# Attention block on one core: the fourth head's probabilities turned by DMA, a ring of five x buffers, the turned norm copied by VectorE

## The chip, the cores and the metric

The kernel runs on one core of a Trainium2 chip. The metric is the device time of one execution in microseconds (us); the value shown is the median of several executions. One more execution was recorded by the hardware profiler, and all rows below come from it.

## What is computed

The input is x, 32 batches of 256 rows by 512, and adj, 32 batches of 256 by 256. For each batch, with 16 heads of width 32:

```
h = max(layernorm(x), 0)
q, k, v = h @ Wq.T, h @ Wk.T, h @ Wv.T            (split into 16 heads)
a = q k^T * 512**-0.5 + 2 * adj                    (per head, 256 x 256)
a = where(any(a != 0, axis=-1), a, -inf); p = softmax(a); p = where(isnan(p), 0, p)
out = x + concat(p v) @ Wo.T
```

The weights are 512 by 512. All data is fp32.

## The kernel before

**The slots.** A batch is called a slot of the pipeline and is cut into 16 steps, one per head (line 541 for ScalarE, 546 and on; each engine has its own `slot` function, and `run`, line 290, calls it for every batch). In a slot the heads of the current batch (`t.cur`) go through softmax, the projections of the next batch (`t.nxt`) are made, and the last group of heads and the output projection of the batch before (`t.prev`) are finished. The order on each engine is written out by hand with these steps. Engines meet only through semaphores.

**Groups of four heads.** The 16 heads form four groups c of four heads j. Head h is 4c + j. Since a PSUM tile has 128 partitions and a head has width 32, four heads of a group share one tile.

- `scores` (PE, L973) makes the logits of a group in four PSUM banks, in step 0, 4, 8 or 12, after the half projection of that step. All operands that matter are pairs of fp16 (`hi` and `lo`), so a product is three matmuls.
- `logit_rows` (VectorE, L683) adds adj and finds the row minimum: three units in step 4c+1, three in step 4c+2, two in step 4c+3 (a unit is half a head).
- `exp_rows` (ScalarE, L492) takes exp into one of four `probs` buffers; `round_probs` (ScalarE, L505) writes the fp16 `hi` part into `p16`, and `split_probs` (GpSimd, L400) the `lo` part. Then the SP queue turns the pair with one DMA transpose (L328) into `pt16`. In step s, ScalarE does exp of head s+2 and the rounding of head s+1, GpSimd the split of head s, and SP issues the transpose of head s-1. This way is taken by heads j = 0, 1, 2 only (`XJ`).
- The fourth head, j = 3 (`YJ`), stays in fp32: `turn_probs` turns it on PE with four transposes (L986) into the PSUM bank `AUX_BANK`, VectorE copies it out (`take_probs_t`, L720), and the product with V is an fp32 matmul (L1020) against `v_y`, an fp32 copy of a part of V that ScalarE makes (L541).
- `values` (PE, L1025 and L1020) multiplies the turned probabilities with V, in steps 4c+7 (that is, steps 3, 7, 11 and 15). Head j writes partitions 32j to 32j+31 of `PV_BANK`, columns 0 to 255.
- The softmax sum: `invert` (VectorE, L700 and L701) makes the reciprocal of the row sums and the row test `some`; `spread_norm` (GpSimd, L409) spreads them; `turn_norm` (PE, L999) turns them into columns 256 to 511 of `PV_BANK`; `take_norm` (ScalarE, L512) copies them to `norm_t`. `values` may only start when that copy is done, since both use the same bank. `take_o` (VectorE, L712) multiplies the two, and GpSimd splits the result (L419, L422).
- `project` (PE, L955) makes half of one of eight projection jobs in each step. `residual` (VectorE, L765) adds the output projection onto `x_res`, in steps 10 and 12.
- `layernorm` (GpSimd, L374 and L380), in step 3, is for the batch after next; `turn_h` (PE, L838) turns its result in steps 5 and 9.

**x and DMA.** All DMAs go out from the SP queue. x of a batch is loaded twice: into `xs` (two buffers) for the norm, and later into `x_res` (two buffers), to which the result is added and from which it is stored (L351).

```
def values(t, d, c):
    for k in range(NX):
        pe.wait_ge(pt16_in[c % 2][k], ...)
    pe.wait_ge(norm_taken, NC * t.batch(d) + (c + 1))
    if NY:
        pe.wait_ge(aux_taken, aux_after("y", t.batch(d), c))
```

## Time and profile before

| | before |
|---|---|
| median of 3 executions | 1099.92 us (1098.54 to 1100.93) |
| the profiled execution | 1103.56 us |
| its span (first to last instruction) | 1101.7 us |
| granted TensorE clock, mean | 0.99 |
| busy time PE | 1071.4 us (97%) |
| busy time ScalarE (ACT) | 923.4 us (84%) |
| busy time VectorE (DVE) | 896.1 us (81%) |
| busy time GpSimd (POOL) | 743.8 us (68%) |
| DMA: data moved | 165.84 MB |

The span is what the profiler's instruction records cover; the execution's own time is 1.9 us longer. A line number (L683) is a line of the kernel before. PE stands for TensorE's matmuls. SPq is the DMA issue queue of SyncE.

### The profile page before, as it was taken

What the parts mean: (1) busy time and instruction counts of PE and PEld (TensorE: products, weight loads), DVE (VectorE), ACT (ScalarE), POOL (GpSimd) and SP (SyncE); (2) the same over time, 40 slices, a digit from 0 to 9 for tenths busy, and PEclk for the clock granted to TensorE, in tenths of its full rate; (3) what the DMA queues carried; (4) which work ended last, traced back from release to release, by engine and by line L of the source; (5) the groups of instructions that cost most, each with busy time, mean ns of one, the idle gap of its engine ahead of it and who ended that gap; (6) DMA issues with size and microseconds to landing.
All of it is one profiled execution on the core that took longest, in us unless ns stands there. A gap on an engine that the chain in (4) does not pass through costs nothing.

```text
span 1101.7 us, 34625 instructions
## 1 busy us (share of the span) xinstructions
PE 1071.4 (97%) x11852; PEld 716.0 (65%) x11852; DVE 896.1 (81%) x3218; ACT 923.4 (84%) x3089; POOL 743.8 (68%) x936
## 2 busy tenths in 40 slices
PE   6789999999999999999999999999999999999987
PEld 5556666666766666666666766666766666666643
DVE  6778888888888888888888888888888888888784
ACT  3488888888888888888888888888988888888884
POOL 1266776677767677677667777667776766767665
PEclk9899999999999999999999999999999999999998
DMA  6167887766777776788877788877777868777866
GB/s 229 39 116 144 161 169 150 159 142 148 156 170 160 150 151 141 153 164 167 146 159 145 153 155 166 156 152 145 150 156 167 159 149 164 133 152 140 139 124 143
DMA packets 443118, 165.84 MB, mean 151 GB/s; under 512 B 408128, under 2 KB 416320, under 8 KB 442944
## 3 DMA queue, kind: packets, MB, share of 16 engines
q1 hardware_dynamic: 442944, 163.64, 73.0%
q8 instruction: 95, 1.56, 0.6%
q14 instruction: 79, 0.65, 0.2%
HBM read 46.14 MB, written 16.78 MB: 57 GB/s over the span
## 4 chain that ended last, share of the span: by engine, by line
PE 93%; DVE 2%; POOL 1%; ACT 1%; DMA 1%; issue 1%; POOLq 0%; SPq 0%; DVEq 0%; ACTq 0%
PE ps L955 60%; PE ps L973 9%; PE ps L1025 6%; PE ps L1020 6%; PE ps L986 5%; PE ps L999 4%; PE ps L838 3%; DVE w_max L603 1%; POOL p L400 1%; DMA w_nat<-in_L_gnn_Wq 1%; ACT probs L492 1%; PE ps L1036 1%; PE ps L850 0%; DMA pt<-p 0%; DVE w_lo L643 0%
## 5 line engine op out<-in xcount | busy, mean ns | idle before, releaser
L400 POOL TENSOR_TENSOR p<-probs,p 128x512 f16<-128x512 f32 x384 | 445.3, 1160 | 301.0 <-ACT p L505 301.0
L683 DVE CUSTOM_DVE_ANT_0 logits<-ps,adj_s,sigma 128x256 f32<-128x256 f32 x1024 | 433.3, 479 | 102.7 <-PE ps L973 102.7
L492 ACT ACTIVATE probs<-logits,row_min 128x256 f32<-128x256 f32 x1024 | 506.3, 500 | 1.2 <-DVE row_min L683 0.7
L955 PE MATMUL ps<-ht_hi,w_hi 128*128 128x256 f16 x1024 | 280.4, 274 | 1.6 <-DVE q_lo L736 1.2
L955 PE MATMUL ps<-ht_hi,w_lo 128*128 128x256 f16 x1024 | 279.7, 273 | 0.0
L955 PE MATMUL ps<-ht_lo,w_hi 128*128 128x256 f16 x1024 | 279.7, 273 | 0.0
L505 ACT ACTIVATE p<-probs 128x512 f16<-128x512 f32 x384 | 237.6, 619 | 0.0
L492 ACT ACTIVATION_READ_ACCUMULATOR probs<-logits,row_min 128x1 f32 x1024 | 198.2, 194 | 0.0
L1020 PE MATMUL ps<-probs_t,v_y 128*32 128x256 f32 x512 | 135.4, 387 | 0.0
L955 PEld LDWEIGHTS ps<-ht_hi,w_hi 128*128 128x128 f16 x1024 | 100.3, 98 | 37.0 <-issue 25.3
L720 DVE COPY probs_t<-ps 128x512 f32<-128x512 f32 x128 | 88.2, 689 | 32.5 <-PE ps L986 32.3
L955 PEld LDWEIGHTS ps<-ht_hi,w_lo 128*128 128x128 f16 x1024 | 100.4, 98 | 11.8
L955 PEld LDWEIGHTS ps<-ht_lo,w_hi 128*128 128x128 f16 x1024 | 100.5, 98 | 11.1
L1025 PE MATMUL ps<-pt,v_hi 128*32 128x256 f16 x1536 | 95.2, 276 | 5.4 <-ACT norm_t L512 3.2
L955 PE MATMUL ps<-w_hi,ht_hi 128*128 128x512 f16 x256 | 98.2, 384 | 0.0
L955 PE MATMUL ps<-w_lo,ht_hi 128*128 128x512 f16 x256 | 98.0, 383 | 0.0
L955 PE MATMUL ps<-w_hi,ht_lo 128*128 128x512 f16 x256 | 97.8, 382 | 0.0
L955 PE MATMUL ps<-w_hi,o_hi 128*128 128x512 f16 x248 | 94.9, 383 | 0.0
L955 PE MATMUL ps<-w_hi,o_lo 128*128 128x512 f16 x248 | 94.5, 381 | 0.0
L955 PE MATMUL ps<-w_lo,o_hi 128*128 128x512 f16 x248 | 94.5, 381 | 0.0
L422 POOL TENSOR_TENSOR o_lo<-o_norm,o_hi 128x256 f16<-128x256 f32 x128 | 86.0, 672 | 10.7
L683 DVE DVE_READ_ACCUMULATOR2_ANT row_min<- 128x1 f32 x1024 | 84.5, 82 | 0.0
(90 smaller groups left out, 1943.2 us busy)
## 6 DMA issues: line engine op xcount, KB each, us to landing
xs<-in_x SPq DMA_DIRECT2D x32, 512.0 KB, 4.0
x_res<-in_x SPq DMA_DIRECT2D x32, 512.0 KB, 3.9
out<-x_res SPq DMA_DIRECT2D x64, 256.0 KB, 2.4
adj_raw<-in_adj SPq DMA_DIRECT2D x32, 256.0 KB, 4.3
pt<-p SPq DMA_TRANSPOSE x384, 3.1
w_nat<-in_L_gnn_Wq SPq DMA_DIRECT2D x1, 1024.0 KB, 6.0
w_nat<-in_L_gnn_Wk SPq DMA_DIRECT2D x1, 1024.0 KB, 8.3
w_nat<-in_L_gnn_Wv SPq DMA_DIRECT2D x1, 1024.0 KB, 10.5
```

The lines of the kernel that those rows point to most:

```text
L400: g.tensor_tensor(p16[:, c % 2, k, 1], probs[:, h % 4].rearrange("p u n -> p (u n)"), p16[:, c % 2, k, 0], ALU.subtract).then_inc(p_split, 1)
L422: g.tensor_tensor(o_lo[:, t.par(d), c, :], o_norm[:, c % 2], o_hi[:, t.par(d), c, :], ALU.subtract).then_inc(o_split, 1)
L492: e = a.activation(probs[:, h % 4, u, :], logits[:, h % 4, u, :], ACT.Exp, bias=row_min[:, t.par(d), u, h:h + 1], scale=-1.0, accum_out=ro ...
L505: a.activation(p16[:, c % 2, k, 0], probs[:, h % 4].rearrange("p u n -> p (u n)"), ACT.Copy)\
L683: v.tensor_tensor_reduce(out=logits[:, h % 4, u, :], in0=ps[:, S_BANK + h % HC, N * u:N * u + N], in1=adj_s[:, t.par(d), u, :], scale=sigm ...
L720: v.tensor_copy(probs_t[:, c % 2, 0], ps[:, AUX_BANK, :].rearrange("p (m n) -> p m n", m=NU))\
L955: m = mm(o, l, r, start=start, stop=stop)
L973: m = mm(ps[:, S_BANK + j, N * u:N * u + N], Q[x][HD * j:HD * j + HD, t.par(d), c, P * u:P * u + P], K[y][HD * j:HD * j + HD, t.par(d), c, ...
L986: m = tr(ps[:, AUX_BANK, N * mh + P * u:N * mh + P * u + P], probs[:, YJ[0], u, P * mh:P * mh + P], ident[:])
L999: m = tr(ps[:, PV_BANK, N + P * u:N + P * u + P], norm[:, c % 2, u, :], ident[:])
L1020: m = mm(o, v_y[:, t.par(d), mh, c, YJ.index(j), :], probs_t[:, c % 2, YJ.index(j), mh, :], start=(mh == 0), stop=(mh == NU - 1))
L1025: m = mm(o, (v_hi, v_lo)[a][:, t.par(d), mh, HD * h:HD * h + HD], pt16[:, c % 2, k, 2 * NU * b + mh:2 * NU * b + mh + NU + 1:NU, :], start ...
```

## The change

- **Heads.** All four heads of a group take the way through fp16, GpSimd and the DMA transpose: `p16` and `pt16` have four heads instead of three. `Y_C`, a list of groups in which the fourth head would still go by PE, is empty, so `turn_probs`, `take_probs_t` and the fp32 matmul issue nothing, and `v_y`, `probs_t` and their copies are gone.
- **GpSimd.** `spread_norm` stands ahead of `split_probs` in its step, where it stood behind it.
- **x.** `xs` is a ring of five buffers. x is loaded once (in step 2 of the slot, for three batches ahead, where it was step 0); `residual` reads and writes the ring buffer, the output is stored from it, and `x_res` and its load are gone.
- **Norm.** `take_norm` moves from ScalarE to VectorE: `tensor_copy`, in steps 4c+2, behind the `logit_rows` of that step.
- **Order.** On VectorE `invert` stands ahead of `logit_rows` in step 4c+3. On PE `turn_h` stands ahead of `values`, `project` and `scores` in its step. On ScalarE `take_h` is in steps 5 and 9, at the end of the step, where it was at the start of steps 6 and 10.

The core of the diff:

```diff
-XJ = (0, 1, 2)
-YJ = tuple(j for j in range(HC) if j not in XJ)
-NX, NY = len(XJ), len(YJ)
+Y_C = ()
+YJ = HC - 1
+X_BEFORE = [sum(not (c in Y_C and j == YJ) for c in range(NC) for j in range(HC) if HC * c + j < h) for h in range(H + 1)]
+X_HEADS = X_BEFORE[H]
+X_RING = 5
...
-        xs = sb("xs", [P, 2, NU, D])
+        xs = sb("xs", [P, X_RING, NU, D])
         xn = sb("xn", [P, NU, D])
-        x_res = sb("x_res", [P, 2, NU, D])
...
-        x_in = [sem(f"x_in{i}") for i in range(2)]
+        x_in = [sem(f"x_in{i}") for i in range(X_RING)]
         adj_in = [sem(f"adj_in{i}") for i in range(2)]
-        xres_in = [sem(f"xres_in{i}") for i in range(2)]
...
-            return (9, 12) if t.first else (6, 10)
+            return (9, 12) if t.first else (5, 9)
...
-                if d is None or h % HC not in XJ:
+                if d is None or not by_dma(h):
                     return
-                c, k = h // HC, XJ.index(h % HC)
-
-                sp.wait_ge(p_split, NC * NX * t.batch(d) + by_dma(h) + 1)
+                c, k = h // HC, h % HC
+
+                sp.wait_ge(p_split, x_count(t.batch(d), h) + 1)
                 need(sp, pv_done, NC * t.batch(d) + (c - 1))
                 sp.dma_start_transpose(pt16[:, c % 2, k], p16[:, c % 2, k].rearrange("p l n -> p (l n)"))\
...
-                    if s == 0 and later(t, 3):
-
-                        sp.wait_ge(xn_ready, NU * t.batch(2))
-                        sp.dma_start(xs[:, t.par(3)], xv[t.batch(3)]).then_inc(x_in[t.par(3)], 16)
                     if s == 0 and later(t, 2):
                         need(sp, adj_scaled, t.batch(1))
                         need(sp, adj_checked, t.batch(1))
                         sp.dma_start(adj_raw[:, t.par(2)], av[t.batch(2)]).then_inc(adj_in[t.par(2)], 16)
-                    if s == 4 and t.cur:
-
-                        sp.wait_ge(out_done[t.par(0)], 16 * NU * t.half(0) + 16 * NU)
-                        sp.dma_start(x_res[:, t.par(0)], xv[t.batch(0)]).then_inc(xres_in[t.par(0)], 16)
+                    if s == 2 and later(t, 3):
+                        b = t.batch(3)
+
+                        need(sp, out_done[b % 2 ^ 1], 16 * NU * ((b - X_RING) // 2 + 1))
+                        sp.dma_start(xs[:, b % X_RING], xv[b]).then_inc(x_in[b % X_RING], 16)
                     if s in (12, 14) and t.prev:
                         u = (s - 12) // 2
                         sp.wait_ge(pj_taken[u], pj_taken_at(t, 4 + u))
-                        sp.dma_start(ov[t.batch(-1)][:, u, :], x_res[:, t.par(-1), u, :])\
+                        sp.dma_start(ov[t.batch(-1)][:, u, :], xs[:, t.batch(-1) % X_RING, u, :])\
                           .then_inc(out_done[t.par(-1)], 16)
...
                 for s in range(H):
-                    split_probs(t, s)
                     if s == 0 and t.prev:
                         spread_norm(t, -1, NC - 1)
                     if s % 4 == 0 and s >= 4 and t.cur:
                         spread_norm(t, 0, s // 4 - 1)
+                    split_probs(t, s)
...
-                b, c, j = t.batch(d), h // HC, h % HC
-                if j in XJ:
-                    need(act, p_split, NC * NX * b + by_dma(h) - NX + 1)
-                elif b + c > 0:
-                    act.wait_ge(aux_full, aux_after(*y_key(b, c - 1)))
+                b, g = t.batch(d), h - HC
+                if g < 0:
+                    b, g = b - 1, g + H
+                if b >= 0 and by_dma(g):
+                    act.wait_ge(p_split, x_count(b, g) + 1)
+                elif b >= 0:
+                    act.wait_ge(aux_full, aux_after("y", b, g // HC))
                 for u in range(NU):
                     act.wait_ge(logits_ready, NU * H * t.batch(d) + (NU * h + u + 1))
                     e = a.activation(probs[:, h % 4, u, :], logits[:, h % 4, u, :], ACT.Exp,
...
                 act.wait_ge(probs_ready, H * t.batch(d) + (h + 1))
-                need(act, pt16_in[c % 2][k], 16 * (2 * t.batch(d) + c // 2))
+                need(act, pt16_in[c % 2][k], 16 * turns_of(t.batch(d), c, k))
                 a.activation(p16[:, c % 2, k, 0], probs[:, h % 4].rearrange("p u n -> p (u n)"), ACT.Copy)\
                  .then_inc(p_hi, 1)
-
-            def take_norm(t, d, c):
-                act.wait_ge(norm_turned, NC * t.batch(d) + (c + 1))
-
-                need(act, o_ready, NC * t.batch(d) + c)
-                a.activation(norm_t[:], ps[:, PV_BANK, N:2 * N], ACT.Copy).then_inc(norm_taken, 1)
...
-                for k, j in enumerate(YJ):
-                    a.activation(v_y[:, t.par(d), u, :, k, :],
-                                 ps[:, PJ_BANK + u, :].rearrange("p (c j d) -> p c j d", c=NC, j=HC)[:, :, j, :],
+                if Y_C:
+                    a.activation(v_y[:, t.par(d), u],
+                                 ps[:, PJ_BANK + u, :].rearrange("p (c j d) -> p c j d", c=NC, j=HC)[:, :, YJ, :],
                                  ACT.Copy, scale=DOWN).then_inc(v_hi_ready, 1)
...
-                    if s == 2 and t.prev:
-                        take_norm(t, -1, NC - 1)
-                    if s % 4 == 2 and s >= 6 and t.cur:
-                        take_norm(t, 0, s // 4 - 1)
-                    if later(t, 2) and s in round_h_steps(t):
-                        k = round_h_steps(t).index(s)
-                        take_h(t, 2, k, aux_after("h", t.batch(2), k))
                     if s == 0 and t.cur:
...
                     exp_rows(t, s + 2)
                     round_probs(t, s + 1)
+                    if later(t, 2) and s in round_h_steps(t):
+                        k = round_h_steps(t).index(s)
+                        take_h(t, 2, k, aux_after("h", t.batch(2), k))
...
+            def take_norm(t, d, c):
+
+                dve.wait_ge(norm_turned, NC * t.batch(d) + (c + 1))
+
+                need(dve, o_ready, NC * t.batch(d) + c)
+                v.tensor_copy(norm_t[:], ps[:, PV_BANK, N:2 * N]).then_inc(norm_taken, 1)
+
...
-                dve.wait_ge(xres_in[t.par(-1)], 16 * t.half(-1) + 16)
-                v.scalar_tensor_tensor(out=x_res[:, t.par(-1), u, :], in0=ps[:, PJ_BANK + u, :],
-                                       scalar=out_scale[:, 0:1], in1=x_res[:, t.par(-1), u, :],
+                v.scalar_tensor_tensor(out=xs[:, t.batch(-1) % X_RING, u, :], in0=ps[:, PJ_BANK + u, :],
+                                       scalar=out_scale[:, 0:1], in1=xs[:, t.batch(-1) % X_RING, u, :],
                                        op0=ALU.mult, op1=ALU.add).then_inc(pj_taken[u], taken_step(t, 4 + u))
...
+                    if s % 4 == 3 and t.cur:
+                        invert(t, 0, s // 4)
                     if s % 4:
                         logit_rows(t, (s + 3) // 4, *LOGITS[s % 4])
-                    if s % 4 == 3 and t.cur:
-                        invert(t, 0, s // 4)
+                    if s == 2 and t.prev:
+                        take_norm(t, -1, NC - 1)
+                    if s % 4 == 2 and s >= 6 and t.cur:
+                        take_norm(t, 0, s // 4 - 1)
...
             def turn_probs(t, d, c):
+                if c not in Y_C:
+                    return
...
-                for k in range(NX):
-                    pe.wait_ge(pt16_in[c % 2][k], 16 * (2 * t.batch(d) + (c // 2 + 1)))
+                for k in range(HC):
+                    if by_dma(HC * c + k):
+                        pe.wait_ge(pt16_in[c % 2][k], 16 * (turns_of(t.batch(d), c, k) + 1))
                 pe.wait_ge(norm_taken, NC * t.batch(d) + (c + 1))
-                if NY:
+                if c in Y_C:
                     pe.wait_ge(aux_taken, aux_after("y", t.batch(d), c))
...
-                        if j in YJ:
-                            m = mm(o, v_y[:, t.par(d), mh, c, YJ.index(j), :],
-                                   probs_t[:, c % 2, YJ.index(j), mh, :], start=(mh == 0), stop=(mh == NU - 1))
+                        if not by_dma(h):
+                            m = mm(o, v_y[:, t.par(d), mh, c, :], probs_t[:, c % 2, mh, :],
+                                   start=(mh == 0), stop=(mh == NU - 1))
                             continue
-                        k = XJ.index(j)
                         for i, (a, b) in enumerate(THREE):
                             m = mm(o, (v_hi, v_lo)[a][:, t.par(d), mh, HD * h:HD * h + HD],
-                                   pt16[:, c % 2, k, 2 * NU * b + mh:2 * NU * b + mh + NU + 1:NU, :],
+                                   pt16[:, c % 2, j, 2 * NU * b + mh:2 * NU * b + mh + NU + 1:NU, :],
...
                         turn_norm(t, 0, s // 4 - 1)
+                    if later(t, 2) and s in turn_h_steps(t):
+                        turn_h(t, 2, turn_h_steps(t).index(s))
...
-                    if later(t, 2) and s in turn_h_steps(t):
-                        turn_h(t, 2, turn_h_steps(t).index(s))
```

Where the instructions stand on three engines, before and now (a line number under "now" is one of the changed kernel). The first place is VectorE at steps 10 and 11 of a slot: the end of a group's logit rows (each unit is the `logits` row and the `row_min` row that reads its accumulator). Before:

```order
L683 ISA logits,row_min<-ps,adj_s,sigma 128x256
L683 ISA row_min 128x1
L683 ISA logits,row_min<-ps,adj_s,sigma 128x256
L683 ISA row_min 128x1
L683 ISA logits,row_min<-ps,adj_s,sigma 128x256
L683 ISA row_min 128x1
L700 RECIPROCAL recip<-row_sum 128x8
L701 SCALAR_TENSOR_TENSOR some<-row_min,some_qk 128x8
L651 SCALAR_TENSOR_TENSOR ht_lo<-ps,ht_hi 128x512
```

Now:

```order
L669 ISA logits,row_min<-ps,adj_s,sigma 128x256
L669 ISA row_min 128x1
L669 ISA logits,row_min<-ps,adj_s,sigma 128x256
L669 ISA row_min 128x1
L706 COPY norm_t<-ps 128x256
L686 RECIPROCAL recip<-row_sum 128x8
L687 SCALAR_TENSOR_TENSOR some<-row_min,some_qk 128x8
L669 ISA logits,row_min<-ps,adj_s,sigma 128x256
L669 ISA row_min 128x1
L669 ISA logits,row_min<-ps,adj_s,sigma 128x256
L669 ISA row_min 128x1
```

The copy of the turned norm (L706) stands behind the sixth logit unit of the group and ahead of `invert` and the last two units; `invert` (recip, some) stood behind all eight. In these steps the residual of step 10 (L765 before, L759 now) stands behind the third of the group's eight units, before and now.

The second place is GpSimd from step 2 to step 5. Before:

```order
L400 TENSOR_TENSOR p<-probs,p 128x512
L374 TENSOR_TENSOR rstd<-var_s,minus_half 128x2
L380 TENSOR_SCALAR xn<-xs,neg_mean,rstd 128x512 x2
L400 TENSOR_TENSOR p<-probs,p 128x512
L409 TENSOR_TENSOR norm<-recip,some 128x256
L400 TENSOR_TENSOR p<-probs,p 128x512
```

Now:

```order
L394 TENSOR_TENSOR p<-probs,p 128x512 x2
L368 TENSOR_TENSOR rstd<-var_s,minus_half 128x2
L374 TENSOR_SCALAR xn<-xs,neg_mean,rstd 128x512 x2
L403 TENSOR_TENSOR norm<-recip,some 128x256
L394 TENSOR_TENSOR p<-probs,p 128x512 x2
```

One split more, that of head 3, stands ahead of `rstd`, and the spread of the norm (L403) is now next behind `xn`, with the split of head 4 behind it instead of ahead.

The third place is PE at step 9 (at step 5 alike), from the end of `scores` (its last 4 matmuls) on. Before, the four transposes of `turn_h` (L838) follow the six or twelve matmuls of the half projection; now (L836):

```order
L971 MATMUL ps<-k_hi,q_lo 128x256 x4
L999 MATMUL ps<-ident,norm 128x128 x2
L836 MATMUL ps<-ident,xn 128x128 x4
L953 MATMUL ps<-ht_hi,w_hi 128x256
```

They stand directly behind `turn_norm` (L999) and ahead of the half projection.

## Rows read from the trace of the kernel before

**Rows 1.** The page, part 1: busy us, share of the span, instructions

```profile
PE 1071.4 (97%) x11852; PEld 716.0 (65%) x11852; DVE 896.1 (81%) x3218; ACT 923.4 (84%) x3089; POOL 743.8 (68%) x936
```

**Rows 2.** The page, part 4: the chain that ended last, by engine

```profile
PE 93%; DVE 2%; POOL 1%; ACT 1%; DMA 1%; issue 1%; POOLq 0%; SPq 0%; DVEq 0%; ACTq 0%
```

**Rows 3.** Chain of waits, one group of four steps: start us, length us, what

```profile
515.77 0.23 PE ps L1025 x3
...
516.78 1.42 PE ps L955 x12
518.20 0.44 PE ps L986 x4
...
519.95 0.77 PE ps L973 x24
...
522.39 0.44 PE ps L838 x4
...
524.14 0.23 PE ps L1025 x3
```

**Rows 4.** Chain of waits: the row tests of two slots, 17 slots apart

```profile
506.36 0.18 PE ps L1036 x8
...
1060.88 0.18 PE ps L1036 x8
```

**Rows 5.** Timeline, PE, one values block: start us, us, line, tiles

```profile
515.70 0.30 PE L1025 MATMUL ps<-pt,v_hi 128*32 128x256 f16 x3
...
516.04 0.40 PE L1025 MATMUL ps<-pt,v_hi 128*32 128x256 f16 x6
...
516.40 0.38 PE L1020 MATMUL ps<-probs_t,v_y 128*32 128x256 f32 x1
```

**Rows 6.** Groups by line, whole span, VectorE and ScalarE: busy us, mean ns

```profile
L505 ACT ACTIVATE p<-probs 128x512 f16<-128x512 f32 x384 | 237.6, 619 | 0.0
...
L720 DVE COPY probs_t<-ps 128x512 f32<-128x512 f32 x128 | 88.2, 689 | 32.5 <-PE ps L986 32.3
...
L712 DVE TENSOR_TENSOR o_norm<-ps,norm_t 128x256 f32<-128x256 f32 x128 | 52.7, 412 | 4.3 <-issue 2.4 <-PE ps L1020 1.8
...
L512 ACT ACTIVATE norm_t<-ps 128x256 f32<-128x256 f32 x128 | 47.4, 370 | 21.3 <-PE ps L999 21.3
```

**Rows 7.** Timeline, VectorE, steps 9 and 10: start us, us, line

```profile
529.12 0.48 DVE L683 CUSTOM_DVE_ANT_0 logits<-ps,adj_s,sigma 128x256 f32<-128x256 f32 x1 [0.79 <-PE ps L973]
...
529.93 0.48 DVE L683 CUSTOM_DVE_ANT_0 logits<-ps,adj_s,sigma 128x256 f32<-128x256 f32 x1
...
530.77 0.75 DVE L765 SCALAR_TENSOR_TENSOR x_res<-ps,out_scale,x_res 128x512 f32<-128x512 f32 x1 [0.35 <-PE ps L955]
531.43 0.47 DVE L683 CUSTOM_DVE_ANT_0 logits<-ps,adj_s,sigma 128x256 f32<-128x256 f32 x1
```

**Rows 8.** Timeline, GpSimd, steps 3 and 4: start us, us, line

```profile
516.22 0.70 POOL L374 TENSOR_TENSOR rstd<-var_s,minus_half 128x2 f32<-128x2 f32 x1 [0.17 <-DVE var_s L597]
...
518.51 1.16 POOL L400 TENSOR_TENSOR p<-probs,p 128x512 f16<-128x512 f32 x1
519.63 0.61 POOL L409 TENSOR_TENSOR norm<-recip,some 128x256 f32<-128x256 f32 x1
```

**Rows 9.** Timeline, ScalarE, step 2: start us, us, line

```profile
514.50 0.60 ACT L521 ACTIVATE q_hi<-ps 128x512 f16<-128x512 f32 x1 [0.17 <-PE ps L955]
...
515.98 0.50 ACT L492 ACTIVATE probs<-logits,row_min 128x256 f32<-128x256 f32 x1
```

**Rows 10.** VectorE's row test (some), all 128: ns min/median/max

```profile
L701 DVE SCALAR_TENSOR_TENSOR some<-row_min,some_qk x128: 110/116/885, 57.5 to 1088.5; 128x8 f32<-128x8 f32 x128
```

**Rows 11.** Windows: a lone transpose, one whole slot: us, PEclk, DMA share, GB/s

```profile
525.00:526.50 1.50, 1.00 0.91 175
500.00:532.62 32.62, 1.00 0.76 155
```

**Rows 12.** DMA transposes, whole span: time from issue to landing

```profile
DMA to landing us min/median/max: 3.0/3.1/5.6
```

More of the change, by code:

```diff
@@ L129, in emit @@
         o_norm = sb("o_norm", [P, 2, N])
[L130 to L132 removed]
+        p16 = sb("p16", [P, 2, HC, 2, NU * N], F16)
+        pt16 = sb("pt16", [P, 2, HC, 4 * NU, P], F16)
         o_hi = sb("o_hi", [P, 2, NC, N], F16)
@@ L180, in emit @@
         p_split = sem("p_split")
-        pt16_in = [[sem(f"pt16_in{i}{k}") for k in range(NX)] for i in range(2)]
+        pt16_in = [[sem(f"pt16_in{i}{k}") for k in range(HC)] for i in range(2)]
         v_hi_ready = sem("v_hi_ready")
@@ L199, in by_dma, with x_count, turns_of @@
         def by_dma(h):
-            return NX * (h // HC) + XJ.index(h % HC)
-        def by_pe(h):
-            return NY * (h // HC) + YJ.index(h % HC)
-        def y_key(b, c):
-            return ("y", b, c) if c >= 0 else ("y", b - 1, NC - 1)
+            return h % HC != YJ or h // HC not in Y_C
+        def x_count(b, h):
+            return X_HEADS * b + X_BEFORE[h]
+        def turns_of(b, c, k):
+            cs = [x for x in range(NC) if x % 2 == c % 2 and by_dma(HC * x + k)]
+            return len(cs) * b + len([x for x in cs if x < c])
         AUX_USES = [("h", 0, 0), ("h", 0, 1)]
         for b in range(-1, NB + 1):
-            slot_uses = [(0, y_key(b, -1)), (4, ("y", b, 0)), (8, ("y", b, 1)), (12, ("y", b, 2)),
+            slot_uses = [(0, ("y", b - 1, NC - 1)), (4, ("y", b, 0)), (8, ("y", b, 1)), (12, ("y", b, 2)),
                          (13, ("row", b + 1))]
@@ L216, in emit @@
             for at, key in sorted(slot_uses):
-                if 0 <= key[1] < NB and not (key[0] == "y" and NY == 0):
+                if 0 <= key[1] < NB and not (key[0] == "y" and key[2] not in Y_C):
                     AUX_USES.append(key)
@@ L394, in split_probs @@
                 d, h = head(t, s)
-                if d is None or h % HC not in XJ:
+                if d is None or not by_dma(h):
                     return
-                c, k = h // HC, XJ.index(h % HC)
-                pool.wait_ge(p_hi, NC * NX * t.batch(d) + by_dma(h) + 1)
+                c, k = h // HC, h % HC
+                pool.wait_ge(p_hi, x_count(t.batch(d), h) + 1)
                 g.tensor_tensor(p16[:, c % 2, k, 1], probs[:, h % 4].rearrange("p u n -> p (u n)"),
@@ L978, in turn_probs @@
             def turn_probs(t, d, c):
+                if c not in Y_C:
+                    return
                 b = t.batch(d)
-                pe.wait_ge(probs_ready, H * b + (HC * c + YJ[0] + 1))
+                pe.wait_ge(probs_ready, H * b + (HC * c + YJ + 1))
                 pe.wait_ge(aux_taken, aux_before("y", b, c))
```

32 lines of the change are left out of this document (13 added, 19 removed).

## The prediction

> **What bounds the kernel now.** I read the busy times first: PE is busy for 97% of the span, ScalarE for 84%, VectorE for 81%, GpSimd for 68% [rows 1]. A busy PE is not yet a bound, so the chain of waits comes next: 93% of what ended last is PE work [rows 2]. The third view is that chain over one group of four steps [rows 3]: `values` follows on projections, transposes and `scores` with no gap. So a microsecond taken off PE is worth a microsecond, until another engine is late for it. The row test comes once a slot, and two of them 17 slots apart give the slot: (1060.88 - 506.36) / 17 = 32.62 us [rows 4].
>
> **What PE loses.** Per group the four fp32 transposes of the probabilities take 0.44 us of the chain [rows 3]. The `values` block takes 516.78 - 515.77 = 1.01 us [rows 3]. In it the three fp16 heads run side by side (three products start together, and the next block half also within 0.4 us), and the last start is the fp32 one [rows 5], so the fp32 strip is what ends it. Now all four heads are fp16, 24 products of 256 columns in four strips. The nearest row for such a block is `scores`, also 24 products in four strips: 0.77 us [rows 3]. Bounds: 0.77 us (as `scores`) and 1.01 us (no gain, the fourth strip costs what the fp32 one did); I take 0.77, because the fp16 strips in rows 5 keep the pace of `scores`. Saved: 0.44 + 0.24 = 0.68 us a group, 2.72 us a slot, and PE alone would need 29.90 us. The Trainium skill (TensorE: Matmul & The Clock Gate, Part 4: PE-mode transpose) puts a 128x128 transpose at about 275 ns in a kernel. By that the four would free 1.1 us a group; the row says 0.44, because they are pipelined, and the row decides.
>
> **What the others gain and lose.** ScalarE gets 128 roundings of 0.619 us and loses 128 norm copies of 0.370 us [rows 6] and the small copies of V: at most +32 us on 923. VectorE loses 128 copies of 0.689 us and gets 128 of 256 columns. That copy has no row; the bounds are 0.37 us (the same copy by ScalarE) and 0.69 us (twice the columns), and I take 0.42, for the VectorE instruction of the same size out of the same bank takes 0.412 us [rows 6]. GpSimd gets 128 splits of 1.16 us [rows 8]: +148 us on 744. None reaches PE's demand in sum. The question is where they stand in the order.
>
> **DMA.** A lone transpose costs 0.91 x 1.5 = 1.37 us of all 16 DMA engines, and a slot now holds 0.76 x 32.62 = 24.8 us [rows 11]. Four more make 30.3 us, less the second load of x, which I can bound only between nothing and a part of those 24.8. So the queues are at most 95% full at my slot below. What matters is landing: 3.1 us in the middle, 5.6 at most [rows 12]. The split of head 3 ends about 2.0 us after the start of `values` in step 3 (below), and its `values` comes a group later, over 8 us after that start. 6 us cover 3.1 and even 5.6: cost nothing. If landing rose above 6, PE would wait for `pt16`. The load of x now waits for a store that was issued four steps earlier: nothing.
>
> **What is late next.** Let E be the end of `scores`. VectorE begins the group's logits there [rows 7]. From E to the next `values` PE has 524.14 - 519.95 - 0.77 = 3.42 us with `turn_h` (0.44 us, steps 5 and 9), 2.98 without (step 1), and 3.16 with the row test (0.18 us, rows 4, step 13) [rows 3]. `values` must wait for the norm copy, which ScalarE did at once and VectorE now does behind six logit units of (529.93 - 529.12) / 2 = 0.405 us each [rows 7].
> 1. Steps 1 to 3: 0.05 + 2.43 + 0.42 + 0.1 for the release = 3.0 against 2.98. Wait 0.05 us. Steps 5 to 7: 3.0 against 3.42, and steps 13 to 15: 3.0 against 3.16, no wait.
> 2. Steps 9 to 11: the residual stands in between. It began 1.65 us behind the first logits, when the half projection was done [rows 7]. `turn_h` now stands ahead of that half, so 2.09 us. Then 0.66 for itself (530.77 to 531.43), 3 x 0.405, 0.42 and 0.15: 4.5 us against 3.42. **PE waits 1.1 us.** Queued behind that wait are this `values`, the projections and the next `scores`; VectorE and ScalarE wait behind those, so all slip together.
> 3. `turn_norm` in step 5 needs GpSimd's spread of the norm. Before, the norm of the layer started 0.52 us behind `values` (515.70) and the spread ended at 520.24, that is 4.54 us behind it, with the split of head 4 in between [rows 5, 8]. Now the split of head 3 comes first. ScalarE can round head 3 when the exps of step 2 are done, 0.28 us behind `values` [rows 9], say 0.2 since `values` is a little later; 0.62 for the rounding [rows 6], 0.07, and the split ends at 2.0 us. The layer's norm thus starts 1.45 us later, the split of head 4 (518.51 to 519.63, 1.12 us) is out of the way, and the spread ends at 4.87. PE arrives at 0.77 + (4.18 - 1.01 - 0.44) + 0.77 = 4.27 us [rows 3]. **PE waits 0.6 us.** Putting the spread first saves 1.12 us of what would have been 1.7.
> 4. The row test `some` on VectorE takes 0.116 us in the middle but 0.885 at most [rows 10]: now and then something holds it for up to 0.77 us. Before each group's logits VectorE was idle 0.79 us [rows 7]. Now PE is 0.68 faster, the 0.61 us pitch of the old copy is gone and 0.34 us of the new one is added: 0.4 us of cover is left. Bounds: nothing, and some 0.5 us in each of three groups. I take 0.3 us a slot, near the low end, since the median hardly waits.
>
> Sum of waits 0.05 + 1.1 + 0.6 + 0.3 = 2.05 us, so a slot takes 31.95 us instead of 32.62. 30 slots have all stages: 30 x 0.67 = 20 us. The slot before them has no residual, and so not the 1.1 us, and gains some 1.8; the end gets one rounding and one split more ahead of its last transpose, 0.62 + 1.16 = 1.8 us. These two cancel. **Forecast: 20 us less.** The profiled execution took 1103.56 us, its span 1101.7; it would take 1083.6. It stands 3.6 us above the median of the runs, so the median becomes 1080.
>
> **The rivals.**
> - *The waits do not bite.* If ScalarE rounds earlier or the residual finds its bank earlier, PE sets the pace: 30 x 2.72 = 82 us less, 1018. With the residual's wait alone, 30 x 1.6 = 48 us less, 1052. For it: the PE chain shows hardly any waits today. Against it: the order puts the copy behind six units, and their time is a plain product. 1018 to 1066 together: 0.15.
> - *The fourth strip is not free.* Place: the `values` block. If it stays at 1.01 us, each slot is 0.96 us longer than forecast, 32.91: 30 x 0.29 = 9 us more than before, 1109, **slower**. It decides from 0.77 + 0.67 / 4 = 0.94 us on. For it: each strip reads its own 128 partitions, which in `scores` it does not. Against: three such strips and the fp32 one ran together in 1.01. 0.10.
> - *GpSimd holds VectorE.* Place: `some` in steps 3, 7, 11, 15, which is moved ahead of the last two logit units while GpSimd has a third more splits. `some` reads two SBUF tiles. Held for the 1.16 us of a split [rows 8], less 0.4 us of cover, it delays logits by 0.7 us, in the two groups without slack at once and in the two others in part: up to 1.5 us a slot instead of my 0.3, 30 x (1.5 - 0.3 - 0.67) = 16 us more, 1116; with half of it, 1098. It decides from 0.97 us a slot on. For it: the 0.885 us. Against: the 0.116 us median. 0.15. The Trainium skill (SBUF — State Buffer, Who interferes with whom) states that a VectorE instruction with two SBUF inputs and a GpSimd instruction that reads SBUF exclude each other for the whole instruction. By that rule each `some` that meets a split is held to its end; whether they meet at all is a matter of phase, and before the change the trace shows that they mostly did not.
> - *The DMA queue fills.* 95% is near; if landing passes 6 us, PE waits. 0.05, around 1100 or more.
>
> **How the numbers follow.** My case, 1066 to 1096 with the sizes of waits 2 to 4 off by half, has 0.55; its middle, 1080, is the prediction. The range leaves out the cheap end of the first rival and the far end of the third: 1048 to 1111. A measurement can tell 0.2%, 2.2 us. Faster: 0.55 + 0.15 + 0.04 of the third rival = 0.74. Within 0.2%: 0.06. Slower: 0.10 + 0.06 + 0.04 = 0.20.
>
> **What would show it.** In the profile after: no fp32 transposes or products in the chain; a `values` block of 0.77 us; PE waiting for VectorE's norm copy some 1.1 us once a slot (about 30 times) and for GpSimd's spread some 0.6 us once a slot; the distance of the row tests 32 us; `some` with a longer mean than 0.17. The forecast is wrong if PE shows no such waits (then near 1018), if the block is near 1.0 us, if `some` is near 1 us in the middle, or if PE waits for a transpose.

## Result and profile after

The changed kernel takes 1086.74 us (median of 4 executions, 1086.49 to 1090.96). The kernel before took 1099.77 us in the same comparison (1098.54 to 1100.93). The ratio is 0.989 with a 95% interval of 0.986 to 0.992: 13 us, or 1.1%, **faster**. The forecast was 1080 us, in a range of 1048 to 1111. The profiled execution took 1090.96 us (span 1089.2), 4 us above the median.

The page of the changed kernel, its parts on busy time, on the DMA queue and on the chain by engine (for [rows 1, 2]):

```profile
PE 996.3 (91%) x11596; PEld 657.4 (60%) x11596; DVE 921.3 (85%) x3218; ACT 937.2 (86%) x3025; POOL 887.8 (82%) x1064
...
q1 hardware_dynamic: 569408, 180.43, 89.0%
...
PE 53%; POOL 19%; DVE 14%; issue 7%; ACT 4%; DMA 1%; POOLq 0%; DVEq 0%; SPq 0%; ACTq 0%
```

PE lost 75 us of work, and the time fell by 13. Before, PE stood for 93% of the chain; now only for 53%. GpSimd (19%) and VectorE (14%), for which PE waits, have most of the rest. The waits of the changed kernel (who waited for what: us in total, times, longest us):

```profile
PE ps L1025 <- DVE norm_t L706: 49.6, 62, 2.7
...
PEld ps L999 <- POOL norm L403: 19.8, 32, 2.0
...
PE ps L999 <- POOL norm L403: 10.3, 30, 1.7
...
PE ps L1025 <- DMA pt<-p: 5.2, 2, 2.7
```

The same on the timeline of PE, over one slot (start us, us, line, in brackets the idle time before it and its releaser). L1025 is `values`, L999 is `turn_norm`; for [rows 3, 5]:

```profile
500.79 0.42 PE L1025 MATMUL ps<-pt,v_hi 128*32 128x256 f16 x8
...
505.23 0.41 PE L999 MATMUL ps<-ident,norm 128*128 128x128 f32 x2
508.59 0.43 PE L1025 MATMUL ps<-pt,v_hi 128*32 128x256 f16 x8 [0.33 <-DVE norm_t L706]
...
513.24 0.44 PE L999 MATMUL ps<-ident,norm 128*128 128x128 f32 x2 [0.30 <-POOL norm L403]
516.67 0.42 PE L1025 MATMUL ps<-pt,v_hi 128*32 128x256 f16 x8
...
520.93 0.44 PE L999 MATMUL ps<-ident,norm 128*128 128x128 f32 x2
525.58 0.43 PE L1025 MATMUL ps<-pt,v_hi 128*32 128x256 f16 x8 [1.19 <-DVE norm_t L706]
...
529.84 0.44 PE L999 MATMUL ps<-ident,norm 128*128 128x128 f32 x2
```

Read it as distances. From `values` to the next `turn_norm` PE needs 4.26 us when nothing is late (516.67 to 520.93, 525.58 to 529.84), and from `turn_norm` to `values` 3.43 us with `turn_h` (513.24 to 516.67). The distances of a slot are above that by 0.18 (500.79 to 505.23), 0.38 (505.23 to 508.59, against the 2.98 without `turn_h` of the kernel before), 0.39 (508.59 to 513.24) and 1.22 us (520.93 to 525.58): 2.17 us of waits. The slot takes 32.20 us, the distance of its row tests (499.20 to 531.41, 32.21), so PE without any waits would take 30.03 us. Before, it was 32.67: the 32.62 read from [rows 4] had the shorter last slot among its 17.

The longest of these waits, on VectorE's timeline of the changed kernel, in steps 10 and 11 (for [rows 7]):

```profile
523.14 0.75 DVE L759 SCALAR_TENSOR_TENSOR xs<-ps,out_scale,xs 128x512 f32<-128x512 f32 x1 [0.78 <-PE ps L953]
523.81 0.47 DVE L669 CUSTOM_DVE_ANT_0 logits<-ps,adj_s,sigma 128x256 f32<-128x256 f32 x1
...
525.02 0.42 DVE L706 COPY norm_t<-ps 128x256 f32<-128x256 f32 x1
```

The residual (L759) idles 0.78 us for its projection. Behind it stand three logit units and then the norm copy, and PE's `values` starts at 525.58, when the copy is done. The copy needs only `turn_norm`, which ended near 521.4.

What the change did to `some`, the row test of the softmax (L687), is told by its durations (ns, min/median/max; for [rows 10]):

```profile
L687 DVE SCALAR_TENSOR_TENSOR some<-row_min,some_qk x128: 109/812/1099, 56.0 to 1075.5; 128x8 f32<-128x8 f32 x128
```

One of them on VectorE's timeline:

```profile
501.66 1.10 DVE L687 SCALAR_TENSOR_TENSOR some<-row_min,some_qk 128x8 f32<-128x8 f32 x1
```

And what GpSimd's timeline has there:

```profile
501.57 1.16 POOL L394 TENSOR_TENSOR p<-probs,p 128x512 f16<-128x512 f32 x1 [2.28 <-ACT p L501]
```

The median went from 116 to 812 ns. The one at 501.66 ends at 502.76, with GpSimd's split that began at 501.57 (ends 502.73). It is no single case: 121 of the 128 take over 0.2 us, and each of these ends within 0.06 us of the end of a GpSimd instruction, 119 times that of a split. That is the rule on two SBUF inputs that the prediction cited (the Trainium skill, SBUF — State Buffer, Who interferes with whom), and the trace agrees with it. It is also where the 0.18 and 0.38 us of that slot come from: VectorE is behind by then, its next `o_norm` begins at 504.68 (PE's `turn_norm` needs the same bank), its logits begin at 505.60, which is after the end of `scores`, and the copy at 508.03. Experiment 4 tests this.

### The profile page after: what moved, and what is told of

It is laid out like the page before. It is cut to its first block, busy times and chain, and to the rows that moved or that the text cites. A ratio compares the mean times of both kernels' runs of the same rounds, so it can differ in the third digit from the quotient of the medians.

```text
span 1089.2 us, 34209 instructions
## 1 busy us (share of the span) xinstructions
PE 996.3 (91%) x11596; PEld 657.4 (60%) x11596; DVE 921.3 (85%) x3218; ACT 937.2 (86%) x3025; POOL 887.8 (82%) x1064
## 4 chain that ended last, share of the span: by engine, by line
PE 53%; POOL 19%; DVE 14%; issue 7%; ACT 4%; DMA 1%; POOLq 0%; DVEq 0%; SPq 0%; ACTq 0%
PE ps L953 35%; POOL p L394 9%; DVE logits L669 7%; PE ps L1025 7%; PE ps L971 5%; POOL xn L374 4%; PE ps L999 3%; PE ps L836 2%; DVE some L687 2%; ACT probs L488 2%; POOL o_lo L416 2%; POOL rstd L368 2%; ACT p L501 2%; POOL norm L403 2%; DVE norm_t L706 1%
## 5 line engine op out<-in xcount | busy, mean ns | idle before, releaser
L394 POOL TENSOR_TENSOR p<-probs,p 128x512 f16<-128x512 f32 x512 | 591.7, 1160 | 145.0 <-ACT p L501 142.1
L501 ACT ACTIVATE p<-probs 128x512 f16<-128x512 f32 x512 | 318.6, 622 | 0.0
L488 ACT ACTIVATION_READ_ACCUMULATOR probs<-logits,row_min 128x1 f32 x1024 | 200.5, 196 | 0.0
L1025 PE MATMUL ps<-pt,v_hi 128*32 128x256 f16 x2048 | 97.8, 278 | 57.2 <-DVE norm_t L706 49.6
L953 PEld LDWEIGHTS ps<-ht_hi,w_hi 128*128 128x128 f16 x1024 | 100.3, 98 | 28.2 <-issue 13.1
L1025 PEld LDWEIGHTS ps<-pt,v_hi 128*32 128x32 f16 x2048 | 52.2, 96 | 100.6 <-issue 100.5
L687 DVE SCALAR_TENSOR_TENSOR some<-row_min,some_qk 128x8 f32<-128x8 f32 x128 | 101.4, 792 | 0.0
L528 ACT ACTIVATE v_hi<-ps 128x512 f16<-128x512 f32 x64 | 38.2, 597 | 71.4 <-PE ps L953 68.6
## 6 DMA issues: line engine op xcount, KB each, us to landing
w_nat<-in_L_gnn_Wv SPq DMA_DIRECT2D x1, 1024.0 KB, 10.9
```

The costliest lines, as they stand in the source:

```text
L394: g.tensor_tensor(p16[:, c % 2, k, 1], probs[:, h % 4].rearrange("p u n -> p (u n)"), p16[:, c % 2, k, 0], ALU.subtract).then_inc(p_split, 1)
L488: e = a.activation(probs[:, h % 4, u, :], logits[:, h % 4, u, :], ACT.Exp, bias=row_min[:, t.par(d), u, h:h + 1], scale=-1.0, accum_out=ro ...
L501: a.activation(p16[:, c % 2, k, 0], probs[:, h % 4].rearrange("p u n -> p (u n)"), ACT.Copy)\
L528: a.activation(v_hi[:, t.par(d), u, :], ps[:, PJ_BANK + u, :], ACT.Copy, scale=DOWN)\
L687: v.scalar_tensor_tensor(out=some[:], in0=row_min[:, t.par(d), :, hs], scalar=0.0, in1=some_qk[:, t.par(d), :, hs], op0=ALU.not_equal, op1 ...
L953: m = mm(o, l, r, start=start, stop=stop)
```

## Experiments

All times are medians; a ratio is to the kernel before in the same comparison. Differences between two experiments are of medians and have no interval of their own.

**1. The copy at the front of its step.** VectorE copies the norm first in steps 4c+2, ahead of the residual and of the last three logit units.

```diff
+                    if s == 2 and t.prev:
+                        take_norm(t, -1, NC - 1)
+                    if s % 4 == 2 and s >= 6 and t.cur:
+                        take_norm(t, 0, s // 4 - 1)
                     if t.prev and s in (10, 12):
...
                         logit_rows(t, (s + 3) // 4, *LOGITS[s % 4])
-                    if s == 2 and t.prev:
-                        take_norm(t, -1, NC - 1)
-                    if s % 4 == 2 and s >= 6 and t.cur:
-                        take_norm(t, 0, s // 4 - 1)
```

> The changed kernel with one move: VectorE copies the turned norm at the start of step 4c+2, ahead of the residual and of three logit units, where it stood behind them. Theory A (PE's waits are what the change gives back): the 49.6 us that PE waits for that copy go, the copy's work stays, and the three units behind it come 0.34 us later; between 35 and 50 us off the changed kernel's 1087, so 1037 to 1052. Theory B (the DMA queues, 94% full in the middle of the run, set the pace): nothing moves, 1084 to 1090. Theory C (VectorE's own chain, with the row test held by GpSimd, is next at once): 10 to 25 us off, 1062 to 1077.

Measured: 1050.14 us (1049.57 to 1052.29), ratio 0.953 [0.952, 0.955]. Its waits have no row of PE for `norm_t`; this one has grown:

```profile
PE ps L999 <- POOL norm L403: 23.8, 33, 1.7
```

49.6 us of waits went and 13.5 came (23.8 against 10.3): 36.1 net, and the median fell by 36.6. The place of one instruction of 0.42 us had taken most of what the change gives: 36.6 us, where the change as it stands gains 13.

**2. The copy back on ScalarE** (`take_norm` as an `activation`, at the start of ScalarE's steps 4c+2; no copy on VectorE).

```diff
-                dve.wait_ge(norm_turned, NC * t.batch(d) + (c + 1))
-
-                need(dve, o_ready, NC * t.batch(d) + c)
-                v.tensor_copy(norm_t[:], ps[:, PV_BANK, N:2 * N]).then_inc(norm_taken, 1)
+                act.wait_ge(norm_turned, NC * t.batch(d) + (c + 1))
+
+                need(act, o_ready, NC * t.batch(d) + c)
+                a.activation(norm_t[:], ps[:, PV_BANK, N:2 * N], ACT.Copy).then_inc(norm_taken, 1)
```

> The changed kernel with one part undone: ScalarE copies the turned norm again, at the start of step 4c+2, as before the change. Theory A: PE's 49.6 us of waits for the copy go and VectorE loses 128 x 0.34 us; ScalarE gets 128 x 0.37 = 47 us on 937 and stays under 1040. 1037 to 1055. Theory B (DMA): no move, 1084 to 1090. Theory D (ScalarE becomes the bound): its rounding of each head slips by up to 0.37 us and GpSimd's chain to turn_norm in step 5 with it, so only 15 to 30 us off, 1057 to 1072.

Measured: 1047.23 us (1045.3 to 1048.4), ratio 0.951 [0.949, 0.953]. Here the engine matters little, the place in its order a lot. (In number 11 the engine does matter.)

**3. GpSimd's spread behind the split again**, the rest as changed.

```diff
+                    split_probs(t, s)
                     if s == 0 and t.prev:
                         spread_norm(t, -1, NC - 1)
                     if s % 4 == 0 and s >= 4 and t.cur:
                         spread_norm(t, 0, s // 4 - 1)
-                    split_probs(t, s)
```

> The changed kernel with one part undone: on GpSimd the spread of the norm stands behind the split of its step again. Theory A: in step 5 PE waits for the spread, which is 1.12 us (a split) later; 30 slots x 1.12 us = 34 us more at most, 20 at least if part of it falls together with the wait in steps 9 to 11: 1107 to 1121. Theory B (DMA sets the pace): within 3 us of 1087.

Measured: 1136.86 us (1135.25 to 1138.52), ratio 1.032 [1.030, 1.034]: 50 us over the changed kernel. A row of its waits:

```profile
PE ps L999 <- POOL norm L403: 61.3, 62, 2.9
```

The two `turn_norm` of one slot that wait, on its timeline of PE:

```profile
503.47 0.44 PE L999 MATMUL ps<-ident,norm 128*128 128x128 f32 x2 [1.41 <-POOL norm L403]
...
511.68 0.44 PE L999 MATMUL ps<-ident,norm 128*128 128x128 f32 x2 [0.45 <-POOL norm L403]
```

The wait in step 5 is 1.41 us where it was 0.30, so 1.11 longer, one split (1.16). But step 9 now waits as well: 62 waits instead of 30, and 61.3 - 10.3 = 51 us, the whole difference. There GpSimd's timeline has a scaling of the adjacency (0.69 us) and a split (1.16) ahead of the spread. The expectation, 1107 to 1121, had counted the first only and was missed.

**4. The row test without SBUF operands from two tensors.** `some` is replaced by a second reciprocal, which has one input. This leaves the row test out.

```diff
-                v.scalar_tensor_tensor(out=some[:], in0=row_min[:, t.par(d), :, hs], scalar=0.0,
-                                       in1=some_qk[:, t.par(d), :, hs], op0=ALU.not_equal, op1=ALU.max)\
-                 .then_inc(norm_step, 1)
+                v.reciprocal(some[:], row_sum[:, t.par(d), :, hs]).then_inc(norm_step, 1)
```

> The changed kernel without the row test: the instruction on VectorE that reads row_min and some_qk (two SBUF tiles) is a second reciprocal of row_sum (one SBUF tile), so the norm is not the reference's; nothing else changes. Theory E (GpSimd's splits hold that instruction: median 0.81 us in the changed kernel against 0.12 before, 87 us over the run): it falls to about 0.2 us each time, and the 8 us by which the changed kernel is slower than I forecast come back, perhaps 15: 1070 to 1080. Theory F (VectorE has slack there): nothing moves in the total, 1084 to 1090, though the instruction is short.

Measured: 1085.28 us (1083.89 to 1086.71), ratio 0.985 [0.984, 0.987]. The instruction takes 0.149 us instead of 0.79, so VectorE has 82 us less to do, and the kernel gains 1.5 us. Two of the waits show why:

```profile
PE ps L1023 <- DVE norm_t L704: 40.3, 33, 3.1
...
PE ps L997 <- POOL norm L403: 18.5, 32, 1.8
```

PE's waits for the copy fell from 62 to 33 and by 9.3 us. Those of steps 1 to 3 are all but gone: the distances that were 0.18 and 0.38 us too long are now 4.27 and 3.12 us, 0.01 and 0.14 too long. So these two were the price of `some`. The wait for the copy in steps 9 to 11 stays, and PE's wait for the spread grew by 8.2 us (18.5 against 10.3). PE reaches `turn_norm` of step 5 earlier, but GpSimd's spread is no earlier, and that wait takes back nearly all of it. The slot went from 32.20 to 32.07 us.

**5. `turn_h` behind the projection and the scores again.**

```diff
-                    if later(t, 2) and s in turn_h_steps(t):
-                        turn_h(t, 2, turn_h_steps(t).index(s))
                     if s == 3 and t.prev:
...
                         scores(t, s // 4 + 1)
+                    if later(t, 2) and s in turn_h_steps(t):
+                        turn_h(t, 2, turn_h_steps(t).index(s))
```

> The changed kernel with one part undone: on PE the transposes of the normed x stand behind the projection and the scores of steps 5 and 9 again. Theory A: the half projection of step 9 ends 0.44 us earlier, so VectorE's residual and the norm copy behind it too, and PE waits 0.44 us less there: 30 x 0.44 = 13 us off, 1070 to 1078. Against it, ScalarE's rounding of the transposes stands at the end of step 5 and 9 and may now wait: then 1080 to 1087.

Measured: 1078.62 us (1077.81 to 1081.09), ratio 0.980 [0.978, 0.983]: 8 us less than the changed kernel. PE's wait for the copy fell to 36.5 us (61 times), 13.1 less, and a usual slot from 32.20 to 31.77 us. The residual finds its projection 0.44 us earlier; that was 0.44 of the 1.22 us. The kernel gains less than the 13 us, and ends just above the expected 1070 to 1078: in the full slots 8 waits for a transpose that landed late cost 4.1 us, where the changed kernel has 3 with 2.0 (how they are told is under number 8).

**6. The fourth head of every group by PE again**, in the changed order.

```diff
-Y_C = ()
+Y_C = (0, 1, 2, 3)
```

> The changed kernel with the fourth head of all groups by PE, VectorE and the fp32 product again (Y_C holds all four groups); the ring, the norm copy on VectorE, the order on GpSimd and PE stay as changed. It takes the change's heads away alone. PE gets 0.44 + 0.2 us a group back, VectorE 0.61 us a group. Theory A: the norm copy is as late after scores as now, so PE's waits for it stay (0.3 and 1.2 us a slot), on top of PE's own 32.6 us: 1125 to 1150, slower than before the change. Theory G (the waits come from the heads alone, from GpSimd and DMA): near the kernel before, 1095 to 1105.

Measured: 1154.26 us (1152.55 to 1155.3), ratio 1.049 [1.047, 1.051]. Two of its waits:

```profile
POOL norm L405 <- DVE some L689: 152.8, 95, 4.5
...
PE ps L1027 <- DVE norm_t L708: 45.8, 34, 3.2
```

So the fourth head by DMA is worth 67.5 us inside the new order, close to PE's 78 us less of work (1074.2 busy here). The other parts alone make the kernel 54 us **slower**; the 1154 us are 4 above the upper end of the expectation. Most of that is PE's wait for the late copy, 45.8 us where the kernel before has 3.2. GpSimd's spread also waits 152.8 us for `some`; what this costs by itself was not separated. The change's 13 us are the difference of two large numbers.

**7. The second load of x put back** as an unread load of 512 KB a slot (as `x_res`, in step 4).

> The changed kernel with a load of x (512 KB) into a buffer that nobody reads, in step 4 of every slot, where the second load stood before: what the ring saves the DMA queues. Theory B (DMA sets the pace): 0.5 MB more a slot on queues 94% full, transposes land later, PE waits for them: 10 to 40 us more, 1097 to 1127. Theory A (waits for VectorE and GpSimd set the pace): transposes have some 3 us of slack, so 0 to 3 us more, 1087 to 1090.

Measured: 1087.97 us (1087.05 to 1088.32), ratio 0.989 [0.987, 0.991]: no difference that these runs could tell, with the queue at 95.2% of its time. The ring of five buffers pays nothing here.

**8. The three cures together:** the copy first (as 1), `turn_h` behind (as 5), and the spread of the first group one step earlier, behind the split of step 3 and ahead of the layer's norm:

```diff
-                    if s % 4 == 0 and s >= 4 and t.cur:
+                    if s % 4 == 0 and s >= 8 and t.cur:
                         spread_norm(t, 0, s // 4 - 1)
                     split_probs(t, s)
+                    if s == 3 and t.cur:
+                        spread_norm(t, 0, 0)
```

> The changed kernel with three moves: the norm copy at the start of step 4c+2 on VectorE; on GpSimd the spread of group 0 in step 3, behind the split of head 3 and ahead of the layer's norm (it stood behind it, in step 4); on PE the transposes of the normed x behind projection and scores. Theory A: PE's waits for the copy (50 us) and for the spread (20 us) both go, what stays is VectorE's chain: 1030 to 1045, ahead of both kernels. Theory C (VectorE's chain with the held row test is next): 1055 to 1070. Theory B (DMA): 1084 to 1090.

Measured: **1038.64 us** (1037.68 to 1040.72), ratio 0.944 [0.942, 0.947], 48 us below the changed kernel and 61 below the one before. Its page:

```profile
PE 988.4 (95%) x11596; PEld 655.3 (63%) x11596; DVE 924.4 (89%) x3218; ACT 936.3 (90%) x3025; POOL 888.1 (86%) x1064
...
PE 80%; DVE 10%; issue 3%; POOL 3%; DMA 2%; ACT 1%; SPq 0%; DVEq 0%; POOLq 0%; ACTq 0%
```

All waits of `values` (L1027) in it (`issue` means that the profile found no releaser within the last us):

```profile
PE ps L1027 <- DMA pt<-p: 9.1, 5, 2.7
...
PE ps L1027 <- DVE k_lo L733: 5.2, 5, 1.5
...
PE ps L1027 <- issue: 4.3, 10, 0.7
```

PE is the bound again. Its slots take 30.24 us at the least, near the 30.03 of PE alone; about half take 0.2 to 1.5 us more, 0.37 us a slot in the mean.

The trace says what these slots wait for, though its labels hide it. In each of the 20 waits above, PE starts 0.24 to 0.40 us after the last of the group's four transposes has landed, whatever the label. The two longest in the full slots: `values` at 584.46 us idles 1.47 us and starts 0.31 us after a transpose that took 6.8 us to land (15 of its 16 completion signals came by 582.61, the last at 584.15); the one at 247.36 idles 1.24 us and starts 0.40 us after one that took 6.5. In the 29 full slots there are 15 such waits with 9.8 us, and these slots together are 10.9 us above 29 times 30.25. So what is left beside PE's own work is nearly all late transposes.

**9. The same with the second load of x** (the edit of 7).

> The kernel 'combo' with the second, unread load of x (512 KB a slot) in step 4. In 'combo' PE is busy for 591 of 600 us in the middle and the DMA share is 1.01, so if the queues can bound this kernel at all, they do here. Theory B (the queue's fill sets the pace once PE no longer waits): 0.5 MB more a slot cost 1 to 2 us a slot, 30 to 60 us, 1068 to 1100. Theory A (a share of 1 is not yet a full queue, since direct and transposing packets overlap): 0 to 6 us more, 1039 to 1045.

Measured: 1045.58 us (1039.57 to 1047.73), ratio 0.949 [0.946, 0.952]. Here the medians differ by 7 us, but the four times spread over 8 us, and the fastest lies among those of number 8; the expectation for a small effect went to 1045. In the full slots late transposes cost 12.2 us in 19 waits, against 9.8 in 15, and one slot takes 34.17 us where the longest of number 8 takes 31.73.

**10. Number 8 without the early spread.**

> The kernel 'combo' without the move of group 0's spread: it stands behind the layer's norm again, in step 4. It tells what the two other moves do by themselves. Theory A: PE waits for the spread in step 5 about 0.7 to 1 us once a slot, as in norm_early (23.8 us by PE over the run): 1058 to 1066 would be all of norm_early's wait plus drains; since the transposes of the normed x now stand behind, I expect 1045 to 1055. If the move of the spread is worth nothing: 1037 to 1040.

Measured: 1054.8 us (1052.92 to 1057.15), ratio 0.958 [0.957, 0.960]. The early spread is worth 16 us. It also shows that with the copy first, `turn_h` behind is no gain but costs some 5 us (1054.8 against the 1050.14 of number 1). A usual slot takes 30.95 us in both, but here late transposes cost 5.9 us in 10 waits, there 2.2 in 4. So number 8 with `turn_h` left in front may be faster still; it was not run.

**11. Number 8 with the copy on ScalarE.**

> The kernel 'combo' with the norm copied by ScalarE as before the change, instead of early by VectorE. VectorE loses 128 x 0.34 us = 44 us and ScalarE gets 128 x 0.37 = 47 us, which brings it to about 983 of 1035. If VectorE's chain is what delays 'combo' here and there: 1030 to 1036, the fastest. If ScalarE at 95% delays the roundings and with them the transposes: 1040 to 1048.

Measured: 1051.64 us (1049.61 to 1053.08), ratio 0.955 [0.953, 0.957], outside both expectations. Number 2 had suggested that ScalarE was the better place; here it loses 13 us. In the full slots late transposes, told as under number 8, cost 16.1 us in 22 waits, 6.3 us more than there, and the fastest slot takes 30.38 us instead of 30.24, some 4 us over the run. The other few us lie ahead of the full slots and behind them. Why transposes land late more often with the copy on ScalarE is not shown.

**12. Number 8 with the edit of 4** (the row test left out again).

> The kernel 'combo' without the row test (a second reciprocal of row_sum stands in its place, one SBUF tile read instead of two), so the norm is not the reference's. In 'combo' the instruction takes 0.833 us in the mean. Theory E (held by GpSimd it costs time once VectorE is 89% busy): 106.7 - 25 = 80 us of VectorE's time free, slots of 31 us and more fall to 30.2, 8 to 12 us off: 1027 to 1031. Theory F (still slack): 1036 to 1040.

Measured: 1039.5 us (1037.16 to 1043.33), ratio 0.945 [0.942, 0.947]: no gain, though `some` takes 148 ns instead of 833. The waits of `values`:

```profile
PE ps L1025 <- DMA pt<-p: 11.6, 9, 2.9
...
PE ps L1025 <- issue: 6.8, 10, 1.9
PE ps L1025 <- DVE k_lo L731: 6.7, 6, 1.5
```

The held row test is not free on PE even here: the fastest slot falls from 30.24 to 30.03 us, which is PE alone. That is 0.21 us a slot, 6.1 us over the 29 full slots. But late transposes now cost 16.0 us in 22 waits there, 6.2 us more than in number 8, and take it all back.

## Why the prediction was right, and where it was off

The mechanism was right: PE saves some 2.7 us a slot, and new waits on VectorE and GpSimd take most of it back. The terms one by one:

- **PE's saving.** Forecast 2.72 us a slot; 32.67 - 30.03 = 2.64 measured. The `values` block took 0.79 to 0.80 us in 125 of the 128 groups, for a forecast of 0.77 [rows 3]. The rival of the fourth strip (1.01) falls.
- **Wait 2, residual then copy:** forecast 1.1, measured 1.22. Experiments 1 and 5 confirm its parts, the place of the copy and the `turn_h` ahead of the projection.
- **Wait 3, the spread in step 5:** forecast 0.6, measured 0.39 by distance. Without the edit to GpSimd's order it would have been one split longer, as argued; that step 9 would then wait too was not seen.
- **Waits 1 and 4 were mis-sized.** Forecast 0.05 for steps 1 to 3 and 0.3 for a held `some`, measured 0.38 + 0.18 = 0.56. What was wrong here is "near the low end, since the median hardly waits": the change moved `some` into the phase in which GpSimd splits, and its median went from 116 to 812 ns. The mechanism of the third rival thus came true, and its price did not: it wanted more than 0.97 us a slot to decide. Leaving the hold out shortens the usual slot by 0.13 us (experiment 4) and the fastest by 0.21 us (experiment 12). The next wait in line takes this back, the spread there and the transposes here, so the medians move by 1.5 us and by nothing.
- **The sum.** 2.17 us of waits against 2.05, and a base of 30.03 against 29.90. That the waits agree so well is partly luck: wait 3 was 0.21 us too large and waits 1 and 4 together 0.21 us too small. With the slot before at 32.67 and not 32.62, the gain is 0.47 us a slot instead of 0.67: 6 us of the 20 over 30 slots.
- **The sum over the run.** The row test of the second slot comes 2.2 us earlier (79.34 against 81.49; forecast 1.8), the 29 distances behind it together give 11.2 us and the last one 0.9, where the forecast had 20; from the last row test to the end it takes 1.7 us more (forecast 1.8). That is the 12.5 us of the span (1101.7 to 1089.2).
- **Two odd slots.** In those 11.2 us, two slots cost 2.1: the row tests at 112.62 and 629.08 come 33.3 us after the ones before them, not 32.2. In both, `values` of step 7 idles some 0.97 us. The trace puts it down to VectorE's `k_lo`, which had ended 0.67 us earlier (at 613.66, `values` at 614.33). Transposes landed late there. Time from issue to landing, in the window 507 to 517 us of a usual slot and 603.5 to 613.5 of an odd one (for [rows 12]):

```profile
DMA to landing us min/median/max: 3.1/3.8/5.4
...
DMA to landing us min/median/max: 3.6/4.0/7.1
```

The 7.1 us belong to the last of the four transposes that this `values` needs. It was issued at 606.97 and landed at 614.02, and PE started at 614.33, 0.31 us later. In the first odd slot `values` starts at 97.87, also 0.31 us after the landing of a transpose, which took 6.6 us. In a usual slot the last one lands 1.8 us before its `values` (514.88, `values` at 516.67). The label `k_lo` is thus wrong, and the waits are for transposes. Both landings are over the 6 us that the prediction set as the limit, so the rival of the DMA queue did happen twice, at 1.1 us each. Why these transposes landed late is not shown. The two waits for `pt` in the table of waits (5.2 us) lie in the last slots (at 1060.98 and 1081.57), behind the last splits.

Two of the prediction's own signs of being wrong came up although the total held: `some` is near 1 us in the middle (0.81), and PE waits for a transpose. And its case of 1066 to 1096 is too narrow for what it says of it: waits 2 to 4 off by half are 1.0 us a slot, 30 us either way, 1050 to 1110.

The first rival (the waits do not bite, 1018 to 1066) is what experiments 1, 2 and 8 reach once the waits are taken away: 1050, 1047 and 1039. Its figure of 1052, for the residual's wait alone being left, is close to the 1050 of experiment 1 by chance: there the copy no longer waits for the residual, and what is left is the wait for the spread.

**Open:** why some transposes take 6 to 7 us to land, and why they do so more often with the copy on ScalarE; whether number 8 is faster with `turn_h` left in front; and whether a row test with one SBUF input would give anything beyond what leaving it out does.

## What to carry over

An instruction that another engine waits for belongs at the front of its step, and its place in the order can be priced beforehand: count the instructions ahead of it by their durations and compare with the time after which the waiting engine arrives. When an engine is relieved, read the slack of all the others first, since the gain stops at the first one that is late; here 48 of 61 possible us stopped there. An edit that gains nothing in the total may still have removed its wait, as in experiments 4 and 12: the distance of one slot tells, the median does not. A change of many parts should be split before it is judged: one part was worth 67 us, the rest cost 54. And a wait can carry the wrong label: compare its end with the landing of the transfers that the instruction also needs.

## What was unexpected of the hardware

- A VectorE instruction of 0.116 us can last up to 1.099 us when GpSimd holds it (a split takes 1.16). It was held 121 times of 128, and removing this moved the median by 1.5 us at most, because another wait took the 0.13 to 0.21 us a slot.
- At a mean DMA share of 1 PE can still be kept busy nearly all the time. The window from 300 to 900 us of the fastest version (us, busy us of PE, PEld, DVE, ACT, POOL, PEclk, DMA share, GB/s):

```profile
300.00:900.00 600.00, 591.47 (x7066) 392.56 (x7064) 555.03 (x1946) 567.23 (x1848) 544.38 (x649) 1.00 1.01 182
```

At a share of 1.01 PE is still busy for 99% of the window; 6.5 of the 8.5 us in which it is not are waits for late transposes. 512 KB more a slot moved the median by 7 us. In the changed kernel the same window has 0.94:

```profile
300.00:900.00 600.00, 564.01 (x6718) 372.47 (x6722) 525.28 (x1845) 537.23 (x1745) 514.28 (x613) 1.00 0.94 173
```

- Four column strips (form 128*32), each reading its own 128 partitions, take PE hardly longer than four row strips (form 32*128), each reading 32: 24 fp16 products of 256 columns in 0.79 us in `values`, and in 0.77 us in `scores` [rows 3].
